# Last mixing step: the count of chosen rows moved ahead of the shared network's second group, and matmuls with no reader while TensorE waits

## The reference: what is computed

```
h = attention(x); h = concat([cls, h])                      # 16 heads of 16
h = h + ssm(layernorm(h))                                   # linear recurrence, then C
x = layernorm(h)
out = h + shared(x)                                         # silu(x Wg) * (x Wu) Wd, inner width 512
probs = sigmoid(x @ Wr.T + rb); scores, idx = top_k(probs, 2)   # of 8 experts
out += sum over the chosen: score * expert_e(x)             # same shape as the shared network
```

## Time and profile before

| | |
|---|---|
| median of 3 runs | 1179.73 us |
| profiled execution | 1175.91 us, span 1174.3 us |
| TensorE (PE) busy | 1117.2 us, 95% |
| VectorE (DVE) busy | 913.8 us, 78% |
| ScalarE (ACT) busy | 590.7 us, 50% |
| GpSimd (POOL) busy | 400.8 us, 34% |
| mean granted TensorE clock | 0.985 of full speed |

### The profile page before, as it was taken

The page is one execution under the profiler, slowest core; times in us unless marked ns, Lnnn a source line. Parts: engine busy times, 40 slices in busy tenths (PEclk is TensorE's granted clock), DMA queues, the critical chain, the costliest instruction groups (busy, mean ns, idle before and its releaser), DMA issues.

```text
span 1174.3 us, 22138 instructions
## 1 busy us (share of the span) xinstructions
PE 1117.2 (95%) x6022; PEld 710.9 (61%) x6023; DVE 913.8 (78%) x1567; ACT 590.7 (50%) x973; POOL 400.8 (34%) x516
## 2 busy tenths in 40 slices
PE   6998999999999999988999999977999999999996
PEld 3654333333333333466777877766888888888885
DVE  3788888888888888589888888777777777777775
ACT  3444777777777777642332221532444444444442
POOL 3011630101111011203454343453555555555553
PEclk9998999999999999999999999988999999999998
DMA  9886232323323233022454431312333333333332
GB/s 295 266 255 210 72 104 70 105 73 93 99 70 106 69 97 86 19 88 75 109 108 108 90 62 49 72 44 71 56 53 54 54 54 54 54 54 54 54 54 32
DMA packets 108691, 105.38 MB, mean 90 GB/s; under 512 B 42464, under 2 KB 97904, under 8 KB 108624
## 3 DMA queue, kind: packets, MB, share of 16 engines
q1 hardware_dynamic: 90528, 81.18, 24.5%
q0 software_dynamic: 18112, 23.57, 11.7%
HBM read 64.88 MB, written 39.68 MB: 89 GB/s over the span
## 4 chain that ended last, share of the span: by engine, by line
PE 70%; DVE 10%; POOL 5%; issue 4%; DMA 1%; ACT 1%; POOLq 0%; DVEq 0%; SPq 0%; ACTq 0%
PE mix_pairs L73 19%; PE by_key L662 11%; PE pv L673 11%; PE by_query L653 9%; PE mix_made L1820 8%; POOL kept_table L1102 4%; PE mix_turn L1807 3%; PE mix_made L1254 2%; PE mix_made L1242 2%; PE mix_turn L1787 1%; PE by_query L694 1%; DVE mix_stats L1432 1%; DVE k_mix_u L1442 1%; DVE mix_h L1428 1%; DVE mix_back L1485 1%
## 5 line engine op out<-in xcount | busy, mean ns | idle before, releaser
L746 DVE TENSOR_REDUCE k_neg_max<-by_query 128x2 f32<-128x1024 f32 x240 | 282.7, 1219 | 54.8 <-PE by_query L653 54.1
L806 ACT ACTIVATE k_wu_e<-by_key 128x512 f32<-128x512 f32 x512 | 278.4, 601 | 84.3 <-PE by_key L662 80.8
L662 PE MATMUL by_key<-k_wg_e 99*128 99x512 bf16 x512 | 180.4, 385 | 3.1 <-DVE pv L782 3.0
L1764 POOL DMA_INDIRECT out_rows<-x_y,k_slot x72 | 113.9, 1582 | 158.6 <-PE mix_turn L1787 109.8
L653 PE MATMUL by_query<-k_wg_e 96*128 96x512 bf16 x480 | 145.2, 383 | 0.2
L1862 ACT ACTIVATE x_gate<-mix_pairs 128x512 f32<-128x512 f32 x72 | 43.0, 597 | 200.9 <-PE mix_pairs L73 200.9
L673 PE MATMUL pv<-k_wu_e,k_wd_e 128*17 128x512 f32 x1024 | 134.5, 598 | 0.3 <-ACT k_wu_e L806 0.3
L662 PEld LDWEIGHTS by_key<-k_wg_e 99*128 99x128 bf16 x512 | 42.4, 97 | 144.2 <-ACT k_wu_e L806 80.8
L73 PE MATMUL mix_pairs<-w_short,x_T 128*128 x288 | 121.8, 423 | 2.0 <-issue 2.0
L1820 PEld LDWEIGHTS mix_made<-x_wd,x_acts_T 128*128 128x128 f32 x864 | 111.2, 188 | 7.4 <-ACT x_acts_T L1885 0.9
L73 PE MATMUL mix_pairs<-w_short,x_rest 128*128 x288 | 114.6, 398 | 0.0
(11 more groups left out here) (244 smaller groups left out, 1947.6 us busy)
## 6 DMA issues: line engine op xcount, KB each, us to landing
k_wg_e<-kept_qk SPq DMA_DIRECT2D x384, 64.0 KB, 2.1
kept_qk<-k_qk_parts SPq DMA_DIRECT2D x32, 384.0 KB, 3.2
kept_v<-k_v_ones SPq DMA_DIRECT2D x8, 544.0 KB, 6.0
k_wd_e<-kept_v SPq DMA_DIRECT2D x32, 136.0 KB, 2.6
k_wu_e<-in_xT POOLq DMA_DIRECT2D x8, 512.0 KB, 6.8
kept_heads<-k_wd_e SPq DMA_DIRECT2D x8, 512.0 KB, 3.0
k_heads_in<-kept_heads SPq DMA_DIRECT2D x8, 512.0 KB, 11.8
k_wg_e<-in_wg_e SPq DMA_DIRECT2D x8, 512.0 KB, 7.8
```

Of the source, the lines that this page charges most:

```text
L662: pe.matmul(by_key[:, key_bank(job), :], k_rows[0:SROWS, g, h, kt * P:(kt + 1) * P], q_rows[0:SROWS, g, h, :], start=True, stop=True).then ...
L746: dve.tensor_reduce(neg_max[:, g % 2, 2 * n:2 * n + 2], by_query[:, bank:bank + 2, :], AX.X, ALU.max, negate=True).then_inc(query_read, 1)
L806: act.activation(probs[:, key_tile(j) // 2 * G + j // 2 % G, j % 2, :], by_key[:, key_bank(job), :], ACT.Exp, scale=float(HD) ** -0.5).the ...
L1764: pool.indirect_dma_start(out=dram["out"], in_=y[:, r % 2, :], in_offset=None, compute_op=ALU.add, out_offset=bass.IndirectOffsetOnAxis(ap ...
```

## The change

Three things change, all on TensorE:

1. In the last step `count` stands right behind the up projection of group 0. Before, the gate of group 1 stood between them.
2. At the end of step 7, behind the turning of u2, 5 matmuls of 128x512 are issued that write to `made[:, 0]` and that nobody reads. A wait for `h2_done` stands in front of them (the earlier readers of that PSUM).
3. At the start of the experts, in front of the first `turn_x`, there are 22 of the same matmuls.

```diff
+        def keep_awake(pe, n):
+            for _ in range(n):
+                pe.matmul(made[:, 0, :], short(w_s_short[:, 0, 0, 0:P]), short(w_s_short[:, 0, 1, :]), start=True, stop=True)
...
                     if not this:
                         shared_up(b - 1, 0, (1,))
-                        shared_up(b - 1, 1, (0,))
                         count(b - 1, nxt)
                     if b == 1:
                         pe.wait_ge(ev["cls_done"], 1)
-                    shared_up(b - 1, 1, (0, 1) if this else (1,))
+                    shared_up(b - 1, 1)
...
                     turn_rows(u2, "u2_turned")
+                    if not nxt:
+                        pe.wait_ge(ev["h2_done"], 2 * B)
+                        mem["keep_awake"](pe, 5)
...
         first = expert(pe, 0)
+        mem["keep_awake"](pe, 22)
         for t in range(2):
             turn_x(0, t)
```

More of the change, by code:

```diff
@@ L989, in stage_mix @@
         slots_out = [sem(f"mix_slots_out{n}") for n in range(2)]
+        def keep_awake(pe, n):
+            for _ in range(n):
+                pe.matmul(made[:, 0, :], short(w_s_short[:, 0, 0, 0:P]), short(w_s_short[:, 0, 1, :]), start=True, stop=True)
+        mem["keep_awake"] = keep_awake
         experts = expert_programs(mem, dram, sem, turn, made, pairs)
```

## The result

The changed kernel took 1173.19 us (median of 9 runs, 1172.19 to 1173.82), the kernel before 1178.12 us beside it (9 runs, 1175.76 to 1181.57). The ratio is 0.9962, 95% interval 0.9949 to 0.9975. It is not the quotient of the two medians (0.9958), so both are given throughout. Forecast was -4.25 us on 1179.73, a ratio of 0.9964. The profiled execution took 1172.59 us, with a span of 1170.9.

A forecast was written before the change was run, and what follows sets the result against it. The prediction took TensorE as the bound, except ahead of the first turning, where GpSimd's scatters and the gather hold it. 2.75 + 1.5 = 4.25 us off 1179.73 gave 1175.5 us, range 1171 to 1181.

The forecast's parts named there:

- Part 1, the count: Last step: the count, moved ahead of group 1's gate, starts 1.50 us earlier with the clock as before.
- rival C: Last step: `place` waits for a scatter, not the count; only 1.5 us gain remains, 1178.2 us; chance 0.03.
- Part 2, the limit by GpSimd's queue: Last step: sequence 7's first scatter follows sequence 6's last by 0.30 us, capping order and 5 matmuls together at 2.75 us.
- Part 2, that the 5 hold the clock: End of step 7: 5 matmuls hold full clock through group 0; 2.75 us with the count's move, 1.50 without the clock.
- Rival A: End of step 7: the five matmuls don't hold the clock, only the order gains; 3.0 us, 1176.7 us; chance 0.15.
- Part 3, the 22: Ahead of the first turning: 22 matmuls speed the first expert tiles; 1.5 us taken, bounds 0 and 2.6.
- What lies behind it: Last step: VectorE's list and the scatters move together, the 8 scatters staying at 13.45 us, +-1 us for another alignment.
- rival D: Last step: scatters fall behind the weight cuts, 2.03 us each; net +2.15 us, 1181.9 us; chance 0.10.
- The sum: Whole chain: 2.75 + 1.5 = 4.25 us off, 1175.5 us on the scale of the median.
- The range: Whole kernel: 1171 to 1181 us, from both gains in full with 3 us of spread, to rival D.

The follow-up runs named there:

- e1_order: Kernel before with only the count moved, without the 5 or 22 matmuls: 1176.88 against 1177.76 us, ratio 0.9988.
- e7_early: Changed kernel plus 5 and 9 unread matmuls in two idle times of step 1: 1172.10 us, ratio 0.9947 to the kernel before.
- e12_eight: Changed kernel with 8 instead of 22 matmuls ahead of the first turning: 1174.93 us, ratio 0.9978 to the kernel before.
- e2_five: Kernel before with only the 5 matmuls at the end of step 7 added, old order: 1178.24 us, ratio 1.0001.
- e3_order_five: Changed kernel without the 22 matmuls, keeping the new order and the 5: 1176.00 us, ratio 0.9995 to the kernel before.
- e10_cuts_late: Changed kernel with three weight cuts (8, 9, 10) moved behind the second shared_add: 1176.85 against 1177.82 us for the kernel before, ratio 0.9987.
- e11_again: Changed kernel run once more with no edit: 1173.05 us, ratio 0.9972 to the kernel before.
- e4_twentytwo: Kernel before with only the 22 matmuls ahead of the first turning added: 1175.61 us, ratio 0.9977.
- e5_order_twentytwo: Changed kernel without the 5 matmuls: 1174.81 against 1177.64 us for the kernel before, ratio 0.9969.
- e6_fill: Changed kernel with 3 more unread matmuls at the last logits, 27 instead of 22, and 4 between the first two turnings: 1174.73 us, ratio 0.9977.
- e8_fill_early: Changed kernel with extra matmuls in step 1 and at the logits, 27 instead of 22, and 4 between the first turnings: 1171.64 us, ratio 0.9954.

## Why the prediction was right, point by point

- **Part 1, the count.** Forecast 1.50 us with the slow clock as before; `e1_order` showed 1.44 at the first scatter. That the count and not a scatter held `place` (against rival C) is shown by the changed kernel: `place` started 0.32 us behind the count at 8.57, long before the time at which the chain had named a DMA (11.7).
- **Part 2, the limit by GpSimd's queue.** Forecast 2.75 us for parts 1 and 2, measured 2.73, and the next bound is the one named: 0.30 us behind sequence 6's last scatter. The 5 cost nothing: the logits began 2.16 us behind the turning, before 2.15. With the clock held the choice itself ended 0.37 us earlier (8.19 instead of 8.56), which the forecast had left fixed; GpSimd's queue hid that.
- **Part 2, that the 5 hold the clock,** is the weak step. It held in 3 of the 7 traces with the plain 5 (the first after, `e7_early`, `e12_eight`) and fell for 3.4 us in 4 (`e2_five`, `e3_order_five`, `e10_cuts_late`, `e11_again`). With 2 or 3 more at the logits it held in 3 of 3. Rival A isn't another outcome of the change but one of some executions. Beside the new order it costs 0.7 to 0.9 us at the first scatter (12.85 to 13.04 against 12.17), not the 1.25 of the prediction. The ratio of the 5 alone shows no gain. They did go with a shorter slow stretch: in the 4 traces without them it was 6.8 us in three (before, `e1_order`, `e4_twentytwo`) and 3.4 in one (`e5_order_twentytwo`), and in the 7 with them never over 3.4.
- **Part 3, the 22.** I took 1.5 us, between 2.4 and 0.6, because I couldn't tell whether the clock would hold. Five traces have exactly the 22 and the weight cuts in their old place. In 4 of them (the first after, `e4_twentytwo`, `e5_order_twentytwo`, `e11_again`) the way from the first turning to `x_acts` was 6.02 to 6.07 us, a gain of 2.3 to 2.4 against 8.38; in the fifth, `e7_early`, 7.58, a gain of 0.8. The mean is 2.0: the term was sized 0.5 us too small. But 8.38 isn't fixed either: without the 22 the way was 8.38, 7.57, 8.75 and 8.36 us in four traces, mean 8.27, and against that the gain is 1.9.
- **What lies behind it.** 13.27 us for the eight scatters against 13.45, so the alignment with the cuts stayed, and rival D didn't come. `e10_cuts_late` shows that its mechanism exists. The Trainium skill says in "SBUF — State Buffer", section "Who interferes with whom", that a VectorE instruction with two SBUF inputs contends with a GpSimd instruction that reads SBUF. The 2.03 us of a scatter beside a cut and the 0.97 us of the same scatter once the cut was moved agree.
- **The sum.** 2.73 + 0.17 + 2.35 = 5.25 us in the trace, with both clocks held, against 4.25 forecast as a mean. The measured medians differ by 4.9 us in the first session and by 4.8 in the last; the ratios give 4.5 (2.9 to 6.0) and 3.3 (1.6 to 5.1). That these lie so near the forecast is in part luck, since two errors cancel. Over the six traces with the new order and the 5, the first scatter came 2.4 us earlier on average, not 2.75, and the 22 gave 1.9 to 2.0, not 1.5.
- **The range.** Its upper end, 1181, was said to reach to rival D, but D's own sum gives 1181.9. It had no bearing here.
- **What I left unexplained,** the 4.7 us spread of the runs before, goes for the most part with the clock. In the 93 timed runs of the kernel before in three sessions, time at half clock (twice the missing share of the mean clock times the span) lay between 30.5 and 52.0 us. A straight line through them gives 0.37 us of time for each us at half clock, with a correlation of 0.83. That is a correlation; the traces show where the time goes. The place of the turning of u2, which no edit but the early ones touched, moved from 768.0 to 774.5 us, and it went with the time at half clock between 500 and 560 us. With 3.4 us of it the turning stood at 768.0 to 768.2 (4 traces), with 6.8 or 10.2 at 769.1 to 770.1 (8 traces), and with 17.1 at 774.4 and 774.5 (2 traces).

Open stays how much of the gain the 5 carry on average. One thing isn't explained: in `e2_five`, VectorE's `place` and ScalarE's next activation both started 1.0 us behind the ends of the matmuls that release them, and no row shows why. Without that the first scatter would have stood at about 14.0 there (an estimate, 14.98 less the 1.0), so that trace isn't a clean measure of the 5.

## What to carry to other kernels

Ask of a wait on TensorE not only what ends it but what follows it: here dense matmuls at half clock cost 0.7 to 0.9 us in front of the count (in the new order) and 1.5 to 2.7 us in the first expert tiles. Matmuls with no reader bought that back in many executions, at no price where they ended before the data came and only where they reached near it. Move the one small product that another queue waits for ahead of the large ones first; that gain came with the clock as low as before, while the filling worked in some executions and not in others. And compare traces from a common event near the change, since slow stretches 240 us earlier went with shifts of all later times by 2 us and more.

## What the runs showed that I had not expected

- The clock falls at another moment in each execution. Behind the same 2.16 us of idleness ahead of the shared network's last part it stayed at 1.00 in the trace before and the first after, and fell for 3.4 us in `e1_order`, `e4_twentytwo`, `e6_fill`, `e8_fill_early` and `e11_again` (2.13 to 2.15 us idle). One trace doesn't prove that a filling holds.
- A slow stretch under matmuls that GpSimd's or VectorE's chain covers costs little: in `e11_again` the clock was low for 3.4 us in the shared network's last part, and the first turning came 22.86 us behind the first scatter instead of 22.61.
- A two-input subtraction of 128x1024 on VectorE and a scatter's issue on GpSimd cost GpSimd up to 1.1 us per meeting (2.03 instead of 0.97), and about as much for gathers (1.87 to 1.96 instead of 0.95).
